# Sixteen-head attention in which the row maxima of two heads come from three products each, in two halves of TensorE's rows

## The reference

```python
q = (x @ wq.T).reshape(B, S, num_heads, D)
k = (x @ wk.T).reshape(B, S, num_heads, D)
v = (x @ wv.T).reshape(B, S, num_heads, D)
scale = 1.0 / jnp.sqrt(jnp.float32(D)).astype(x.dtype)
scores = jnp.einsum('bqhd,bkhd->bhqk', q, k) * scale
probs = jax.nn.softmax(scores, axis=-1)
out = jnp.einsum('bhqk,bkhd->bqhd', probs, v).reshape(B, S, H)
```

## Time and profile before

| | |
|---|---|
| time, median of 3 runs | 7174.47 us (7169.87 to 7174.76) |
| the profiled execution, its own time | 7183.58 us |
| its span | 7181.8 us |
| PE busy | 5763.3 us (80%), 26178 matmuls |
| weight loads busy | 3029.1 us (42%) |
| DVE, ACT, POOL busy | 4253.9 (59%), 2749.3 (38%), 1762.4 us (25%) |
| mean granted TensorE clock | 0.888 |

### The profile page before, as it was taken

The page is one execution under the profiler, slowest core; times in us unless marked ns, Lnnn a source line. Parts: engine busy times, 40 slices in busy tenths (PEclk is TensorE's granted clock), DMA queues, the critical chain, the costliest instruction groups (busy, mean ns, idle before and its releaser), DMA issues. The chain is left out here.

```text
span 7181.8 us, 69269 instructions
## 1 busy us (share of the span) xinstructions
PE 5763.3 (80%) x26178; PEld 3029.1 (42%) x26194; DVE 4253.9 (59%) x7193; ACT 2749.3 (38%) x4376; POOL 1762.4 (25%) x2107
## 2 busy tenths in 40 slices
PE   7969999999877865656566687899694887799966
PEld 4435555555534432323222255332582444433344
DVE  5664454444365469898998922777225765587622
ACT  4543333333204333333333321567112555456500
POOL 2211121211013015353444500220204213222022
PEclk9989999999888987888787886899797998899988
DMA  1000000000000000000000000000351000000022
GB/s 45 1 2 1 1 1 1 1 1 1 18 9 17 7 24 0 0 0 0 0 0 0 0 9 15 22 1 1 109 182 33 1 15 1 27 1 1 26 92 86
DMA packets 47884, 134.60 MB, mean 19 GB/s; under 512 B 4822, under 2 KB 31990, under 8 KB 41534
## 3 DMA queue, kind: packets, MB, share of 16 engines
q1 hardware_dynamic: 38094, 77.67, 3.1%
q0 software_dynamic: 9456, 52.50, 2.1%
HBM read 99.42 MB, written 31.20 MB: 18 GB/s over the span
## 5 line engine op out<-in xcount | busy, mean ns | idle before, releaser
L73 PE MATMUL PS<-SC 128*32 128x512 f32 (+12 forms) x11760 | 2703.7, 464 | 625.9 <-DVE SC L82 500.6
L79 ACT ACTIVATE SC<-PS 128x512 f32<-128x512 f32 (+10 forms) x2773 | 1900.8, 716 | 1967.2 <-PE PS L73 1622.1
L94 DVE TENSOR_REDUCE SC<-PS 128x1 f32<-128x512 f32 (+4 forms) x2832 | 1567.5, 594 | 697.4 <-PE PS L73 682.6
L73 PEld LDWEIGHTS PS<-SC 128*32 128x32 f32 (+5 forms) x11760 | 988.7, 122 | 1933.9 <-DVE SC L82 617.1
L73 PE MATMUL PS<-AR 128*128 128x512 f32 (+6 forms) x3902 | 1219.0, 424 | 106.9 <-DVE SC L82 55.2
L82 POOL TENSOR_TENSOR SC<-SC 128x128 bf16<-128x128 f32 (+4 forms) x764 | 935.2, 1232 | 1070.5 <-ACT SC L79 749.3
L76 PE MATMUL PS<-AR,SC 128*104 128x128 bf16 (+4 forms) x4820 | 579.4, 265 | 499.9 <-DVE SC L85 228.4
L73 PE MATMUL PS<-SC,AR 128*128 128x512 f32 (+7 forms) x1824 | 861.1, 602 | 61.9 <-DVE SC L82 20.6
L91 DVE TENSOR_TENSOR_SCAN SC<-SC 128x512 f32<-128x512 f32 (+1 forms) x544 | 885.7, 1689 | 14.9 <-ACT SC L79 3.5
L73 PEld LDWEIGHTS PS<-AR 128*128 128x128 f32 (+2 forms) x3902 | 631.7, 178 | 529.9 <-issue 334.3
L79 ACT ACTIVATE SC<-SC 128x512 f32<-128x512 f32 (+5 forms) x874 | 440.5, 561 | 1015.4 <-DVE SC L91 741.7
(11 more groups left out here) (71 smaller groups left out, 2049.5 us busy)
## 6 DMA issues: line engine op xcount, KB each, us to landing
xg<-AR SPq DMA_DIRECT2D x20, 512.0 KB, 5.4
SC<-in_pk11e SPq DMA_DIRECT2D x8, 1152.0 KB, 6.5
SC<-in_pk11e SPq DMA_DIRECT2D x8, 1028.0 KB, 5.1
SC<-xg SPq DMA_DIRECT2D x23, 256.0 KB, 2.9
yg<-SC SPq DMA_DIRECT2D x23, 256.0 KB, 2.2
SC<-xg SPq DMA_DIRECT2D x8, 512.0 KB, 6.1
yg<-SC SPq DMA_DIRECT2D x8, 512.0 KB, 3.3
AR<-in_pk SPq DMA_DIRECT2D x2, 1562.0 KB, 8.5
```

The source lines that it names most:

```text
L73: return Step(self.real and self.real.matmul(*a, **k))
L79: return Step(self.real and self.real.activation(*a, **k))
L94: return Step(self.real and self.real.tensor_reduce(*a, **k))
```

## The change

The six blocks of a head are put in another order, so that the three largest products (middle by high, high by middle, high by high) come first: q's blocks now hold middle, high, high, high, low, middle and k's high, middle, high, low, high, middle. Odd heads have them in reverse and 16 columns further right, in a tile `ST` of 112 columns for 104. Turned, an even head has its three largest products on partitions 0 to 47, an odd head on partitions 64 to 111. The maxima are computed from these three alone, over 48 rows; the score keeps all six, over 98 rows for even heads and 112 for odd ones (whose maximum rows are 0 and 1).

A piece `max` is now a pair of heads: two matmuls, one behind the other, the first in rows 0 to 47 and the second in rows 64 to 111 of TensorE (tiles of 64 rows at 0 and 64), into two banks, with one semaphore step at the end. Mask products follow in the full shape. DVE reduces the two banks one after the other, in cross-attention too. The banks 5, 6, 7 are given in turn as before, and a pair takes two turns; PE waits for both before the first of its matmuls. The banks of the scores are now named by a turn as well, and are the same as before (0, 1 and 2, 3).

Since even and odd heads lie apart, ACT, DVE and POOL write the parts in two instructions where one did, except the high parts of k, which were two instructions and are two. To make room, three small buffers move: the statistics of the norm of stage 0, and a row and a zero tile of stage 11.

```diff
+        self.ST = [scr.take([2, 8, 112], BF16) for _ in range(3)]
         self.A = [scr.take([2, 8, 16]) for _ in range(3)]
         self.Oc = scr.take([512])
...
+        self.ring, self.rings, self.turns = {}, ([], []), {}
+        for p in self.first:
+            self.queue(p)
+        for n in range(len(self.steps)):
+            for jj in range(2):
+                self.queue(("score", n, jj))
+                for p in self.slots[2 * n + jj]:
+                    self.queue(p)
+        self.queue(("out", len(self.units) - 1))
+
+    def queue(self, p):
+
+        if p[0] == "turn":
+            self.turns[p] = len(self.turns)
+        if p[0] != "fin1":
+            z = 0 if p[0] == "score" else 1
+            for q in [p + (0,), p + (1,)] if p[0] == "max" else [p]:
+                self.ring[q] = (z, len(self.rings[z]))
+                self.rings[z].append(q)
+
+    def read_by_act(self, p):
...
     def max_pieces(self, u):
-        return [("max", u, i, half) for i in range(16 if self.KV == S else 8) for half in range(self.halves(u))]
+        return [("max", u, qt, jj, half) for qt in range(4) for jj in range(2) for half in range(self.halves(u))]
 
     def tiles(self, u):
 
...
 
     def bank(self, p):
-        return 5 + self.use[p] % 3
+        z, n = self.ring[p]
+        return 2 * (n % 2) if z == 0 else 5 + n % 3
 
     def turn_on_act(self, p):
...
     def wait_bank(self, e, p):
 
-        n = self.use[p] - 3
+        z, n = self.ring[p]
+        n -= (2, 3)[z]
         if n >= 0:
-            self.wait_read(e, self.by_use[n])
+            self.wait_read(e, self.rings[z][n])
 
     def wait_turned(self, e, s):
...
         return divmod(n, len(self.work))
 
-    def slot(self, ST, rows, z, js):
-        v = ST[0:rows, z, :, 0:96].rearrange("p h (j d) -> p h j d", d=16)
+    def slot(self, ST, rows, z, odd, js):
+
+        v = ST[0:rows, z, odd:8:2, 16 * odd:16 * odd + 96].rearrange("p h (j d) -> p h j d", d=16)
+        js = sorted(5 - j for j in js) if odd else js
         if len(js) == 1:
             return v[:, :, js[0], :]
         return v[:, :, js[0]:js[-1] + 1:js[1] - js[0], :]
...
             s, g, qb = self.units[u]
             b, qS, kS = s // 2, self.qS[s % 2], self.kS[s % 2]
-            o = self.max_bank(p)
+            o = [self.max_bank(p, k) for k in range(2)]
+            w = o[0].shape[1]
+            q0, k0 = 512 * qb + 128 * qt, 512 * half
+            diag = self.causal and half == self.halves(u) - 1
             self.wait_turned(e, s)
-            if self.KV == S:
-                qt, j = i // 4, i % 4
-                h, q0 = 4 * g + j, 512 * qb + 128 * qt
-                diag = self.causal and half == self.halves(u) - 1
-                m = e.matmul(o, qS[0:QH, h, q0:q0 + 128], kS[0:QH, h, 512 * half:512 * half + o.shape[1]], start=True, stop=not diag)
+            self.wait_bank(e, p + (1,))
+            for k, r in ((0, slice(0, 48)), (1, slice(64, 112))):
+                h = 4 * g + 2 * jj + k
+                m = e.matmul(o[k], qS[r, h, q0:q0 + 128], kS[r, h, k0:k0 + w], start=True, stop=not diag and self.mask is None)
+            for k in range(2):
+                if self.mask is not None:
+                    m = e.matmul(o[k], K.identb, self.mask[0][:, 8 * b + 4 * qb + qt, :], start=False, stop=True)
                 if diag:
-                    m = e.matmul(o[:, o.shape[1] - 128:o.shape[1]], K.identb, K.maskS, start=False, stop=True)
-            else:
-                qt, jj = i // 2, i % 2
-                q0 = 512 * qb + 128 * qt
-                for k in range(2):
-                    h = 4 * g + 2 * jj + k
-                    m = e.matmul(o[:, KC * k:KC * k + KC], qS[0:QH, h, q0:q0 + 128], kS[0:QH, h, 0:KC], start=True, stop=self.mask is None)
-                    if self.mask is not None:
-                        m = e.matmul(o[:, KC * k:KC * k + KC], K.identb, self.mask[0][:, 8 * b + 4 * qb + qt, :], start=False, stop=True)
+                    m = e.matmul(o[k][:, w - 128:w], K.identb, K.maskS, start=False, stop=True)
             m.then_inc(K.mm, (tag, p))
         elif p[0] == "fin2":
...
-            h = 4 * g + 2 * jj + k
-            o = PS[0:rows, 2 * jj + k, lo:512]
-            m = e.matmul(o, self.kS[s % 2][0:QM, h, 128 * t:128 * t + rows], self.qS[s % 2][0:QM, h, q0 + lo:q0 + 512], start=True,
+        self.wait_bank(e, ("score", n, jj))
+        for j in (2 * jj, 2 * jj + 1):
+            h, r = 4 * g + j, (QM, 112)[j % 2]
+            bank = K.PS[0:rows, self.bank(("score", n, jj)) + j % 2, :]
+            m = e.matmul(bank[:, lo:512], self.kS[s % 2][0:r, h, 128 * t:128 * t + rows], self.qS[s % 2][0:r, h, q0 + lo:q0 + 512], start=True,
                          stop=not diag and self.mask is None)
...
-                m.then_inc(K.av, (tag, "hi" if not hk else "hi q", s, w))
-            if hk:
-                e.activation(self.slot(ST, rows, 1, [0, 3]), self.dup(a[:, 1], rows, 2), ACT.Copy).then_inc(K.av, (tag, "hi k", s, w))
-                e.activation(self.slot(ST, rows, 1, [5]), a[0:rows, 1], ACT.Copy).then_inc(K.av, (tag, "hi", s, w))
+            for odd in range(2):
+                if hq:
+                    e.activation(self.slot(ST, rows, 0, odd, [1, 2, 3]), self.some(a, rows, 0, odd, 3), ACT.Copy).then_inc(
+                        K.av, (tag, "hi" if odd and not hk else ("hi q", odd), s, w))
+                if hk:
+                    e.activation(self.slot(ST, rows, 1, odd, [0, 2, 4]), self.some(a, rows, 1, odd, 3), ACT.Copy).then_inc(
+                        K.av, (tag, "hi" if odd else "hi k", s, w))
         elif p[0] == "turn" and self.turn_on_act(p):
             self.turn_out(e, p)
...
-            _, u, i, half = p
-            o, m2 = self.max_bank(p), self.m2[u % 2]
+            _, u, qt, jj, half = p
             e.wait_ge(K.mm, (tag, p))
-            if self.KV == S:
-                e.tensor_reduce(m2[:, i // 4, i % 4, half:half + 1], o, AX.X, ALU.max).then_inc(K.vv, (tag, "aux", p))
-            else:
-                e.tensor_reduce(m2[:, i // 2, 2 * (i % 2):2 * (i % 2) + 2, 0], o.rearrange("p (k n) -> p k n", k=2), AX.X,
-                                ALU.max).then_inc(K.vv, (tag, "aux", p))
+            for k in range(2):
+                e.tensor_reduce(self.m2[u % 2][:, qt, 2 * jj + k, half:half + 1], self.max_bank(p, k), AX.X, ALU.max).then_inc(K.vv, (tag, "aux", p + (k,)))
         elif p[0] == "fin1":
             u = p[1]
             m2, Mst = self.m2[u % 2], self.Mst[u % 2]
-            e.wait_ge(K.vv, (tag, "aux", self.max_pieces(u)[-1]))
...
-            e.tensor_copy(self.slot(ST, rows, 1, [1, 4]), self.dup(a[:, 1], rows, 2)).then_inc(K.gv, (tag, "mid k", s, w))
-        if hq:
-            e.wait_ge(K.gv, (tag, "mid q", s, w))
-            m = e.tensor_tensor(self.slot(ST, rows, 0, [5]), a[0:rows, 0], self.slot(ST, rows, 0, [3]), ALU.subtract)
-            m.then_inc(K.gv, (tag, "lo q" if hk else "parts", s, w))
-        if hk:
-            e.wait_ge(K.gv, (tag, "mid k", s, w))
-            e.tensor_tensor(self.slot(ST, rows, 1, [2]), a[0:rows, 1], self.slot(ST, rows, 1, [1]), ALU.subtract).then_inc(K.gv, (tag, "parts", s, w))
+        for odd in range(2):
+            if hq:
+                e.tensor_copy(self.slot(ST, rows, 0, odd, [0, 5]), self.some(a, rows, 0, odd, 2)).then_inc(K.gv, (tag, "mid q", odd, s, w))
+            if hk:
+                e.tensor_copy(self.slot(ST, rows, 1, odd, [1, 5]), self.some(a, rows, 1, odd, 2)).then_inc(K.gv, (tag, "mid k", odd, s, w))
+        e.wait_ge(K.gv, (tag, "mid k" if hk else "mid q", 1, s, w))
+        for odd in range(2):
+            if hq:
+                m = e.tensor_tensor(self.slot(ST, rows, 0, odd, [4]), self.some(a, rows, 0, odd, 1), self.slot(ST, rows, 0, odd, [0]), ALU.subtract)
+                m.then_inc(K.gv, (tag, "parts" if odd and not hk else ("lo q", odd), s, w))
+            if hk:
+                m = e.tensor_tensor(self.slot(ST, rows, 1, odd, [3]), self.some(a, rows, 1, odd, 1), self.slot(ST, rows, 1, odd, [1]), ALU.subtract)
+                m.then_inc(K.gv, (tag, "parts" if odd else "lo k", s, w))
 
     def pool(self, e):
         for p in self.first:
```

More of the change, by code:

```diff
@@ L516, in place @@
         self.first = self.prep(0) + self.max_pieces(0) + [("fin1", 0), ("fin2", 0)]
[L517 to L527, removed]
+        self.ring, self.rings, self.turns = {}, ([], []), {}
[16 more added lines that the diff above has]
+    def read_by_act(self, p):
+        return (p[0] == "split" and self.bias is None and not self.has_post) or (p[0] == "turn" and self.turn_on_act(p))
     def spread(self, pieces, a, b, rank=0):
@@ L560, in wait_read @@
         K, tag = self.K, self.tag
-        on_act = (p[0] == "split" and self.bias is None and not self.has_post) or (p[0] == "turn" and self.turn_on_act(p))
-        e.wait_ge(K.av if on_act else K.vv, (tag, "aux", p))
+        if p[0] == "score":
+            e.wait_ge(K.av, (tag, "exp", p[1], p[2]))
```

(36 more changed lines are left out.)

51 lines of the change are left out of this document (21 added, 30 removed).

## The result

The changed kernel takes 7557.97 us (median of 4 runs, 7555.20 to 7560.74); before, on the same chip, 7174.61. The ratio is 1.0531, 95% interval 1.0513 to 1.0550: slower by 383 us, where 172 had been forecast. The span of the profiled execution grew from 7181.8 to 7553.2 us, its mean granted clock fell from 0.888 to 0.858.

The account below looks back on a forecast made before the run. PE, hanging on DVE once per step for a free bank, was taken as the bound. Terms 38 + 50 + 45 + 31 + 8 = +172 on 7183.58 gave 7355, 7345 for timed runs; range 7235 to 7450.

Parts of the forecast that it names:

- The step that failed: Attention stages: granted clock of the three shown 0.92 to 0.98, so nearly all runs at 2.4 GHz.
- 2, `a8` and `a11`: Two stages: a pair waits for two banks before its first product, unit 26.94 against 25.68; +38 us, bounds 0 to +80.
- 3, `a0` and `a9`: Triangle self-attention: mask products after a shape change delay the reduce, 0.2 for each of 128 pairs; +50 us.
- 4, `a10`: Cross-attention with masks: two banks and two reduces per pair, 0.89 from pair to pair; +45 us.
- 4, `a4`: Cross-attention without mask product: two banks and two reduces, 0.66 a pair, +1.9 a unit; +31 us.
- 5, preparation: Parts of a tile on POOL, ACT, DVE: more, smaller instructions, some 1.5 us per stage, six stages; +8 us.
- Streaming saved: Maximum pairs on PE: two products run at once, saving 190 us against 150 us of shape changes if all exposed.
- B: Maximum pairs: the two halves don't overlap, the pair streams as before and pays the shape changes; 7480, chance 0.08.
- C: Slot behind the scores: banks free early enough, PE stays the bound and its saving counts; faster, 7143, chance 0.07.
- D: Around the maximum products: changes to 64 rows nearly free, only the way out exposed; 7285, chance 0.10.
- hardly higher: Sign in the changed profile: DVE's busy share of the six attention stretches hardly higher, its idle time higher.

Follow-up runs that it names:

- rows 0:48: Kernel before, with each maximum product contracting only rows 0 to 47, which adds array shape changes; one-bank maxima kept: 7456.09 us, ratio 1.0399.
- rows 0:66: Kernel before, with each maximum product contracting rows 0 to 65 in the array's full shape, no shape change added: 7211.32 us, ratio 1.0045.
- rows 0:80: Kernel before, with each maximum product contracting rows 0 to 79 in the array's full shape: 7190.70 us, ratio 1.0024.
- 112 rows: Kernel before, with maxima and scores contracting rows 0 to 111, the added rows zero on the query side, same results: 7167.77 us, ratio 0.9992.
- two short fillers: Changed kernel, with the first head's product repeated one to three times between the two bank waits, contracting 48 or 96 rows: 7581.53 and 7522.63 us.
- own waits: Changed kernel, but each product of a pair waits for its own bank and signals on its own, each reduce waits for its product: 7458.06 us, ratio 1.0394.
- full rows: Changed kernel with a wait, signal and bank per product and products over rows 0 to 95 and 0 to 111: 7321.83 us, ratio 1.0200.
- layout alone: Changed kernel's layout of the parts with the plan, banks and full-shape one-bank maxima of the kernel before: 7188.25 us, ratio 1.0018.
- full-row pair kernel: Changed kernel with its pair plan and wait for both banks, but products over rows 0 to 95 and 0 to 111, no overlap: 7612.11 us, ratio 1.0606.
- the square above: Four pair-plan kernels: with a wait per product, 7322 (full rows) and 7458 (48 rows); with the wait for both banks, 7612 and 7558.
- filler with 96 rows: Changed kernel, with the first head's product repeated one to three times over rows 0 to 95 between the two bank waits: 7522.63 us, ratio 1.0484.

## Why the prediction was right or wrong

The direction held, and in the main the mechanisms that the sum names; the size was less than half, mainly because a term is missing.

**The step that failed** is the first paragraph: "the granted clock of the three shown is 0.92 to 0.98, so nearly all of it runs at 2.4 GHz". That was true of before and was carried over to after without being asked again; every term of the sum stands at 2.4 GHz, and the clock is a term put at nothing. What the runs showed in its place is 648 us at 1.2 GHz for 133, worth some 167 of the 371 us by which the profiled spans differ. What a low-clock microsecond costs in a dense stretch is in the run with rows 0:48: four steps that follow in `a0` at 1.2 GHz, and their counterparts in `a9` at 2.4 GHz:

```profile
357.28:391.58 34.30, 34.30 (x159) 15.42 (x158) 16.17 (x33) 11.20 (x19) 8.27 (x20) 0.50 0.00 1
5941.15:5964.31 23.16, 21.08 (x147) 9.10 (x145) 18.20 (x42) 10.17 (x17) 7.38 (x19) 1.00 0.00 1
```

(34.30 - 23.16) / 34.30 = 0.325 of the time. Checked against runs that change rows alone: rows 0:66, 120 us more low clock x 0.325 = 39, the six stages +40; rows 0:80, 64 x 0.325 = 21, stages +22; 112 rows, -24 x 0.325 = -8, stages -8. In the pair plan it holds for `a0` of the two short fillers: 164 x 0.325 = 53, measured 53. For the changed kernel 515 x 0.325 = 167 us. That is an estimate: where PE waits at 1.2 GHz, the microsecond may cost less, which no run prices. It leaves 371 - 167 = 204 of the spans' difference for the terms that were forecast at 172:

| term | forecast | stages longer | of it clock (x 0.325) | left |
|---|---|---|---|---|
| 2, `a8` and `a11` | 38 | 76 | 16 | 60 |
| 3, `a0` and `a9` | 50 | 142 | 101 | 41 |
| 4, `a10` | 45 | 72 | 20 | 52 |
| 4, `a4` | 31 | 71 | 31 | 40 |
| 5, preparation | 8 | 10 | - | 10 |

1. *Streaming saved*: the overlap is real, 3 to 6 ns between the starts. But with own waits, 48-row halves lose 136 us against full rows (7458 for 7322): 1629 changes of shape and 344 us more low clock outweigh what is streamed less. With the wait for both banks they win 54; there the shorter stream is inside the chain.
2. *Two banks*: steps 3.13, 4.40, 3.54, 1.97, 3.80 for 3.04, 4.24, 3.53, 1.96, 3.85; unit 27.50 for 26.94. Right in kind, 0.1 short per waiting pair. 30 units of +1.82 (27.50 for 25.68) are 55 of the 60 us, so the units in which the next segment is prepared, taken "at the same mean", add little; the term, 38, was a third too small.
3. *`a0`, `a9`*: the part without the clock, 41, is near the forecast's 50, and partly by luck: the 50 is the mask products' alone, and the 0.45 read for each dense step (8.35 to 8.8) never went into the sum. The clock is more than twice as much.
4. *Cross-attention*: without the clock a little short, 0.98 from pair to pair in `a10` for 0.89. The chain in the sum holds one reduce of 0.31 per pair, the one that frees a bank, and that a second reduce by itself costs nothing fits it. That the bank is the cause is what is left, not shown.
5. *Preparation*: right (layout alone 13 us by the medians, interval 6 to 20).

Rivals: B falls, the products overlap. C falls by the square above: even with own waits the halves lose. D falls: at 512 columns a 98-row matmul behind a 48-row one starts 318 ns after it, a 112-row one 220 to 227 behind a 98-row one of the same shape, 0.09 to 0.10 for the change; and with rows 0:48 in the kernel before, the way out (a 48-row one behind a 98-row one) is 312 ns, so both ways cost 0.09 to 0.10, the way back too, which the prediction had no row of this kind for. Of the signs, DVE's busy share of the six stretches fell, 0.69 to 0.61, where "hardly higher" was written.

The trace of before held a hint. In `a4`, where PE was busy 143 of 177 us, the clock was 0.92, low five times; in `a10`, with 191 of 213, it was 0.98, low once at the start: a change that makes PE wait more in dense stretches had to be asked about the clock. The Trainium skill, TensorE: Matmul & The Clock Gate, A second HAM failure mode: psum-queue depth-cycling, says that short idle times between groups of matmuls that turn through PSUM banks make the clock swing between its levels. The full-row pair kernel agrees with it (no added shape change, PE idle for banks, low clock 560 us against 236 with own waits). Idle time isn't all of it: with rows 0:66 PE was as busy ahead of the fall as before, and the clock stayed low longer.

**What stays open.** How rows, idle time and drains are weighed; why `a8` keeps 0.95 to 0.97 under the same edits that bring `a0` to 0.76; whether rows that hold zeros count in full (the run with 112 rows suggests that they count, within its error). A pair into one bank from both row halves, which would spare the second bank in the cross-attentions, wasn't tried; the Trainium skill, TensorEngine Tiling (Array Packing), Gotcha 1: PSUM Pressure, says that different row tiles can't access the same bank at once, which no run here shows.

## What to carry to other kernels

Ask of every change in a PE-dense stretch what it does to the granted clock, and put a price on it: here 0.33 us for each us at 1.2 GHz in dense steps, by that estimate nearly half of the whole loss. Half the rows in two halves of the array is no free halving: at 512 columns 0.21 us saved stood against two changes of shape of 0.09 and a lower clock. And if one consumer empties a small ring of banks, a unit of work that takes two banks at once costs a wait that the faster matmul didn't repay: +100 us here with the short products, +290 with the long.

## What had not been expected of the hardware

- At equal columns, shape and plan, contracting fewer rows lowers the granted clock in dense stretches: low-clock time 109, 133, 197, 253 us for 112, 96, 80, 66 rows; time 7168, 7175, 7191, 7211 us. The first step is not clear of noise.
- Added matmuls can make a kernel faster: filler with 96 rows -35 us against none. The same with 48 rows is +24, with intervals that overlap.
- Two row halves start 3 to 6 ns apart, and the change of shape to or from full rows costs 0.09 to 0.10 us at bf16, like the 0.09 of the earlier trace rows.
